# A windowed-attention network on one core: one pipeline over all tiles, a transposed attention product, normalisation moved to another engine

## The chip, the core and the metric

The kernel runs on one core of a Trainium2 chip. A core has five engines with instruction streams of their own: TensorE (PE, matrix products into PSUM), VectorE (DVE), ScalarE (ACT), GpSimd (POOL) and SyncE (SP, here for DMAs). They meet at semaphores. The metric is the device time of one execution in microseconds. About 0.5% is what a measurement of this kernel can tell from no change.

## What is computed

Three parts: a retention layer, a network of six layers of windowed attention with gated FFN, and a second layer with attention and a mixture of experts. The change is in the network alone, on x of shape (4, 512, 128):

```python
for i in range(DEPTH):                        # 6
    x = attn_layer(shift_tokens(x), Wqkv[i], q_scale[i], k_scale[i], Wo[i]) + x
    x = ffn_layer(shift_tokens(x), ln_g[i], ln_b[i], W1[i], b1[i], W2[i], b2[i]) + x
...
def attn_layer(x, Wqkv, qs, ksc, Wo):         # 16 heads of 64
    q, k, v = jnp.split(x @ Wqkv, 3, -1)
    q = l2norm(q) * qs
    k = l2norm(k) * ksc
    q = q * cos * scale + rotate_half(q) * sin * scale
    k = k * cos * inv + rotate_half(k) * sin * inv
    out = local_attention(q, k, v)            # windows of 32 queries, 64 keys
    return out @ Wo
...
sim = jnp.einsum('bhwie,bhwje->bhwij', bq, bk2) * QK_SCALE
attn = jax.nn.softmax(jnp.where(mask, -jnp.finfo(sim.dtype).max, sim), -1)
out = jnp.einsum('bhwij,bhwje->bhwie', attn, bv2)
...
return a * jax.nn.gelu(gate, approximate=False) @ W2 + b2
```

Everything is f32 but the mask product, which is bf16.

## The kernel before

`build_retention` runs first, then `build_network`, then `build_second_layer`; each is a block of its own. In `build_network` the unit of work is a tile of 128 tokens. A batch has four tiles (`s` or `t`, 0 to 3), a round is one layer of one batch, and there are 6 x 4 = 24 rounds, 96 tiles. A round's four stages handle tile `s` at lag 0, and work of earlier tiles at lag 1 and 2 (`Round.tile`). One stage of TensorE (`pe_round`) has:

- at lag 0, the projections: four matmuls of 512 columns for q and k into `qk_ps` (L393), two for v into the ring (L380);
- at lag 1, sixteen transposes of the normalised `qkn` in four bursts (L404), the mask product (L418) and the scores (L423), 64 small matmuls in two halves, into `sc_ps`;
- at lag 2, eight transposes of the exponentials `pe_` (named `pexp` in the profile, L438), the attention product (L453) in two halves, also into `sc_ps`, and eight transposes of its normalised output `o_tok` (L467).

In the attention product the stationary operand is `prT`, 64 keys by 32 queries of one head, and the moving one is `v_win`, 64 keys by 64 columns. Its output has the queries on the partitions, so it is transposed before the output projection.

VectorE (`dve_round`) rotates q and k out of `qk_ps` (L708, L713), sums the squares that ScalarE made (L721), floors them (L726), does a Newton step on the inverse norms (`newton_step`, L733 to L737), takes maxima and subtracts them (L742, L747), sums the exponentials and takes the reciprocal (L755, L757), and multiplies the attention output by it (`normalise`, L767). GpSimd adds the two rotary terms in two halves (L352) and multiplies by the inverse norms in two halves (L359). ScalarE copies what comes out of the ring (L564), squares (L575), makes the exponentials (L613) and the inverse norms (L580, L584), and runs GELU (L603), for which it loads another table and then the first one again. SyncE loads weights and moves V into windows, 16 DMAs per tile.

All transposes, v and the FFN go through `ring`, two PSUM banks filled in turn in the order of a list written out by hand (`order`); `bank_free` makes each fill wait for the reader of the fill two before. The FFN of round r runs in round r + 1: the output projection (L475, eight matmuls of 512 columns, each of two records), `add_attention` (L776), centring and variance (L481, L486) in stage 2; the up projections of gate and linear part (L493, L495), GELU, `ffn_gated` (L789), the down projection (L502) and `add_ffn` (L796) in stage 3. `ffn_norm` (L781, L783) ends stage 2 on VectorE.

A matmul of f32 shows as two records, a transpose as one. PSUM tile `sc_ps` is used in turn: scores of tile t (lag 1), maxima and subtraction on VectorE, attention product of tile t (lag 2, next stage), `normalise` on VectorE, scores of the next tile. The waits on both sides are these two lines, in `scores` and in `attend`:

```python
pe.wait_ge(o_ready.sem, o_ready.at(it, 2 * t))
...
pe.wait_ge(sc_sub.sem, sc_sub.at(it, 2 * (t + 1)))
```

## Time and profile before

| | us |
|---|---|
| runs of the kernel before: lowest, median, highest of 3 | 2250.7, 2259.16, 2259.73 |
| the profiled execution: its own time | 2256.97 |
| its span, first to last instruction | 2255.2 |
| mean granted TensorE clock | 0.972 of full |
| TensorE busy (matmul) | 1958.2 (87%) |
| VectorE busy | 1561.8 (69%) |
| ScalarE busy | 1151.2 (51%) |
| GpSimd busy | 863.9 (38%) |

The busy time of TensorE counts matmuls that overlap once, and their modelled ends; the distance between the starts of two successive groups is the better measure of what a group costs. In a timeline row the columns are start, duration, engine, line, operation, output<-inputs, stationary shape, moving shape, number of records, and in brackets the idle time ahead of the first of them with what ended it.

### The profile page before, as it was taken

The numbers are of one execution on the slowest core, as the hardware profiler recorded it, in microseconds if no ns is written. First come the engines' busy times: TensorE is split into PE (matmuls) and PEld (weight loads), VectorE is DVE, ScalarE is ACT, GpSimd is POOL, SyncE is SP. The second block draws the span as 40 slices with busy tenths as digits, with TensorE's granted clock in tenths as the row PEclk, the third lists the DMA queues.
The fourth block names the chain that finished last, engine by engine and source line by source line (L and its number), as shares of the span: only waits on it lengthen the run. The fifth ranks groups of instructions, "written<-read, shape, count | busy, mean of one in ns | idle before, by whom it ended". The sixth has DMA issues, their size and how long they took to land. (4 is left out here: it accounts for less than half of the span.)

```text
span 2255.2 us, 71087 instructions
## 1 busy us (share of the span) xinstructions
PE 1958.2 (87%) x31016; PEld 1121.9 (50%) x31016; DVE 1561.8 (69%) x2095; ACT 1151.2 (51%) x1934; POOL 863.9 (38%) x427
## 2 busy tenths in 40 slices
PE   6858889889989898989889898899988888986898
PEld 5635455455545544554555454455544545543444
DVE  6648777777767877777777777778777777863443
ACT  4425555554655555455555555555555555553234
POOL 0225444444434534444443444444445444430000
PEclk9979999999999999999999999999999999997788
DMA  1023222223222322222232222232223222221000
GB/s 42 1 72 93 48 54 60 73 58 75 54 46 56 87 66 58 55 51 67 62 79 50 57 57 74 49 75 62 50 56 86 66 49 56 60 52 43 0 9 10
DMA packets 83885, 124.96 MB, mean 55 GB/s; under 512 B 26112, under 2 KB 31880, under 8 KB 82704
## 3 DMA queue, kind: packets, MB, share of 16 engines
q1 hardware_dynamic: 83600, 120.64, 22.2%
q8 instruction: 242, 3.96, 0.8%
q14 instruction: 43, 0.35, 0.1%
HBM read 21.98 MB, written 1.05 MB: 10 GB/s over the span
## 5 line engine op out<-in xcount | busy, mean ns | idle before, releaser
L352 POOL TENSOR_TENSOR t<-t 128x1024 f32<-128x1024 f32 x192 | 453.3, 2361 | 661.4 <-DVE t L713 661.4
L359 POOL TENSOR_TENSOR qkn<-t,rn 128x1024 f32<-128x1024 f32 x192 | 374.2, 1969 | 373.9 <-DVE rn L737 373.9
L393 PE MATMUL qk_ps<-wqkv,state 128*128 128x512 f32 x768 | 396.5, 599 | 11.5 <-DMA wqkv<-in_w_qkv 9.2
L708 DVE TENSOR_TENSOR t<-qk_ps,rot 128x1024 f32<-128x1024 f32 x192 | 234.5, 1222 | 195.4 <-ACT sq L575 135.5
L404 PEld LDWEIGHTS ring<-ident,qkn 128*128 128x128 f32 x1536 | 180.9, 141 | 198.9 <-issue 122.0
L404 PE MATMUL ring<-ident,qkn 128*128 128x128 f32 x1536 | 233.8, 278 | 26.2 <-POOL qkn L359 25.6
L713 DVE TENSOR_TENSOR t<-qk_ps,rot 128x1024 f32<-128x1024 f32 x192 | 233.1, 1214 | 0.0
L721 DVE TENSOR_REDUCE lnsum<-sq 128x16 f32<-128x1024 f32 x192 | 231.8, 1208 | 0.0
L564 ACT COPY prT<-ring 128x512 f32<-128x512 f32 x192 | 113.2, 590 | 217.2 <-PE ring L438 217.2
L575 ACT ACTIVATE sq<-qk_ps 128x1024 f32<-128x1024 f32 x192 | 198.0, 1031 | 39.0 <-PE qk_ps L393 38.0
L564 ACT COPY oT<-ring 128x512 f32<-128x512 f32 x192 | 112.6, 586 | 184.0 <-PE ring L467 184.0
L380 PE MATMUL ring<-wqkv,state 128*128 128x512 f32 x384 | 200.4, 624 | 3.6 <-DMA wqkv<-in_w_qkv 2.7
L423 PE MATMUL sc_ps<-kT,qT 64*32 64x64 f32 x12288 | 170.6, 224 | 23.9 <-issue 23.9
L423 PEld LDWEIGHTS sc_ps<-kT,qT 64*32 64x32 f32 x12288 | 135.9, 105 | 83.1 <-issue 82.8
L475 PE MATMUL ring<-oT,wo 128*128 128x512 f32 x384 | 170.7, 598 | 0.7 <-ACT oT L564 0.7
L453 PE MATMUL sc_ps<-v_win,prT 64*32 64x64 f32 x12288 | 168.1, 225 | 2.7 <-issue 1.6
L564 ACT COPY v_tok<-ring 128x512 f32<-128x512 f32 x192 | 112.1, 584 | 113.3 <-PE ring L380 113.3
L453 PEld LDWEIGHTS sc_ps<-v_win,prT 64*32 64x32 f32 x12288 | 135.6, 106 | 63.9 <-issue 62.3
L564 ACT COPY qT<-ring 128x512 f32<-128x512 f32 x192 | 111.4, 580 | 104.7 <-PE ring L404 104.7
L742 DVE TENSOR_REDUCE smax<-sc_ps 128x16 f32<-128x1024 f32 x96 | 117.2, 1221 | 68.1 <-PE sc_ps L423 68.1
L438 PE MATMUL ring<-ident,pexp 128*128 128x128 f32 x768 | 120.0, 279 | 29.5 <-ACT pexp L613 20.4
L438 PEld LDWEIGHTS ring<-ident,pexp 128*128 128x128 f32 x768 | 87.8, 140 | 111.0 <-issue 74.7
(235 smaller groups left out, 2727.2 us busy)
## 6 DMA issues: line engine op xcount, KB each, us to landing
v_win<-v_tok SPq DMA_DIRECT2D x1488, 64.0 KB, 2.0
wqkv<-in_w_qkv SPq DMA_DIRECT2D x6, 1024.0 KB, 5.6
wqkv<-in_w_qkv SPq DMA_DIRECT2D x6, 512.0 KB, 3.7
wo<-in_w_o SPq DMA_DIRECT2D x6, 512.0 KB, 3.8
w<-in_w SPq DMA_DIRECT2D x6, 341.0 KB, 4.0
w<-in_w SPq DMA_DIRECT2D x6, 192.0 KB, 3.9
r_xtok<-in_x SPq DMA_DIRECT2D x4, 256.0 KB, 4.0
amask<-in_att_mask SPq DMA_DIRECT2D x1, 1024.0 KB
```

The costliest lines, as they stand in the source:

```text
L352: nc.gpsimd.tensor_tensor(t1[:, to], t1[:, to], t2[:, to], ALU.add).then_inc(qk_added.sem, 1)
L359: nc.gpsimd.tensor_tensor(qkn[:, to].rearrange("p (h d) -> p h d", d=DH), t1[:, to].rearrange("p (h d) -> p h d", d=DH), rn[:, HEADS * hal ...
L380: nc.tensor.matmul(to, tile_of(r, s), wqkv[:, 2 * INNER + 512 * par:2 * INNER + 512 * (par + 1)], start=True, stop=True).then_inc(v_full.s ...
L393: nc.tensor.matmul(qk_ps[:, c, :], tile_of(r, s), wqkv[:, 512 * c:512 * (c + 1)], start=True, stop=True).then_inc(qk_full.sem, 1)
L404: ins = nc.tensor.transpose(to[:, n * P:(n + 1) * P], qkn[:, c * P:(c + 1) * P], ident[:, :])
L423: ins = nc.tensor.matmul(sc_ps[WIN * q:WIN * (q + 1), par, 64 * pair:64 * (pair + 1)], qT[64 * par:64 * (par + 1), pair, WIN * q:WIN * (q ...
L438: ins = nc.tensor.transpose(to[:, n * P:(n + 1) * P], pe_[:, c * P:(c + 1) * P], ident[:, :])
L453: ins = nc.tensor.matmul(sc_ps[WIN * q:WIN * (q + 1), par, DH * pair:DH * (pair + 1)], prT[64 * par:64 * (par + 1), pair, WIN * q:WIN * (q ...
L564: nc.scalar.copy(to, bank_of(r, (what, s, lag, f))).then_inc(done.sem, 1)
L708: nc.vector.tensor_tensor(t1[:, to].rearrange("p (h d) -> p h d", d=DH), own, rot[:, 2 * half, s:s + 1, :].to_broadcast([P, HEADS, DH]), A ...
L713: nc.vector.tensor_tensor(t2[:, to].rearrange("p (h s d) -> p h s d", s=2, d=DH // 2), swapped, rot[:, 2 * half + 1, s:s + 1, :].to_broadc ...
L721: nc.vector.tensor_reduce(lnsum[:, HEADS * half:HEADS * (half + 1)], sq[:, INNER * half:INNER * (half + 1)].rearrange("p (h d) -> p h d", ...
```

## The change

The order by rounds becomes one loop over stages g = 0 to 101, in Python on every engine, so that GpSimd's and SyncE's instruction streams are written out too. Stage g has the projections of tile g, the qkn transposes and scores of tile g - 1, the P transposes of g - 2 and the attention product of g - 3. Row maxima and row sum of tile g - 2 stand at the head of VectorE's stage g.

The FFN of a round is spread over stages (by g modulo 4): up projections with GELU in 0, down projection and first half of the output projection (now two halves of 256 columns) in 1, second half in 2, centring, variance and norm in 3.

The attention product has `v_win` (64 keys by 64 columns) as its stationary operand and `prT` (64 keys by 32 queries) as its moving one, and writes head columns by queries, straight into the two ring banks; ScalarE copies them to `oT`. `transpose_o`, `o_tok` and `normalise` are gone. In their place GpSimd multiplies the exponentials by `rden` ahead of the transposes (`scale_p`, two halves of 512 columns).

The Newton step and the floor are on GpSimd (`inverse_norms`, five operations on 128x32), which also scales q and k in four quarters of 512 columns where it did two halves; ScalarE makes its own floored copy (`raised`, one more small activation). The rotary tables have two buffers. The output projection's weights are loaded apart from the FFN's.

TensorE's order at the end of a plain stage and the head of the next, before (L467 transposes `o_tok`, L418 is the mask product, L453 is the attention product):

```order
L380 MATMUL ring<-wqkv,state 128x512 [waits qkT_copied] x2
L418 MATMUL sc_ps<-mask_bf,ident_bf 128x512 [waits o_ready,qkT_copied]
L418 MATMUL sc_ps<-mask_bf,ident_bf 128x512
L423 MATMUL sc_ps<-kT,qT 32x64 x32
L467 MATMUL ring<-ident,o_tok 128x128 [waits v_copied,o_ready]
L467 MATMUL ring<-ident,o_tok 128x128 x3
L423 MATMUL sc_ps<-kT,qT 32x64 x32
L467 MATMUL ring<-ident,o_tok 128x128 [waits v_copied,o_ready]
L467 MATMUL ring<-ident,o_tok 128x128 x3
L393 MATMUL qk_ps<-wqkv,state 128x512 [waits q_sq]
```

and in the change, at the end of a stage with g modulo 4 = 1 and the head of the next (L423 transposes `pn`, L404 is the mask product, L409 the scores, L440 the attention product, L370 and L379 project q and k, L392 transposes qkn):

```order
L404 MATMUL sc_ps<-mask_bf,ident_bf 128x512 [waits sc_sub,qkT_copied]
L404 MATMUL sc_ps<-mask_bf,ident_bf 128x512
L409 MATMUL sc_ps<-kT,qT 32x64 x32
L423 MATMUL ring<-ident,pn 128x128 [waits v_copied,p_scaled]
L423 MATMUL ring<-ident,pn 128x128 x3
L409 MATMUL sc_ps<-kT,qT 32x64 x32
L440 MATMUL ring<-prT,v_win 64x32 [waits pT_copied,v_moved3]
L440 MATMUL ring<-prT,v_win 64x32 x31
L370 MATMUL qk_ps<-wqkv,state 128x512 [waits q_rot,q_sq]
L440 MATMUL ring<-prT,v_win 64x32 x32
L370 MATMUL qk_ps<-wqkv,state 128x512
L392 MATMUL ring<-ident,qkn 128x128 [waits oT_copied,qk_scaled]
```

The P transposes moved to the place of the output's, the attention product to the head of the stage; the scores wait for the subtraction (`sc_sub`) where they waited for `o_ready`.

GpSimd's work for one tile, before:

```order
L352 TENSOR_TENSOR t<-t 128x1024 [waits qk_rot]
L350 REGISTER_ALU
L352 TENSOR_TENSOR t<-t 128x1024 [waits qk_rot]
L353 REGISTER_ALU
L354 REGISTER_ALU [waits qk_added]
L359 TENSOR_TENSOR qkn<-t,rn 128x1024 [waits qkT_full,rn_ready]
L359 TENSOR_TENSOR qkn<-t,rn 128x1024
```

and in the change, from one stage's inverse norms on:

```order
L295 TENSOR_SCALAR ss<-sums 128x32 [waits sums_ready]
L297 TENSOR_TENSOR nw<-rs 128x32 [waits rs_ready]
L299 TENSOR_TENSOR nw<-nw,ss 128x32 [waits newton]
L301 TENSOR_SCALAR nw<-nw 128x32 [waits newton]
L303 TENSOR_TENSOR rn<-nw,rs 128x32 [waits newton]
L311 TENSOR_TENSOR qkn<-qkn,rn 128x512 [waits q_added,rn_ready]
L311 TENSOR_TENSOR qkn<-qkn,rn 128x512
L311 TENSOR_TENSOR qkn<-qkn,rn 128x512 [waits k_added]
L311 TENSOR_TENSOR qkn<-qkn,rn 128x512
L328 TENSOR_TENSOR pn<-pexp,rden 128x512 [waits pT_full,rden_ready]
L328 TENSOR_TENSOR pn<-pexp,rden 128x512
L320 TENSOR_TENSOR qkn<-t 128x1024 [waits qkT_full,q_rot]
```

Four instructions for a tile became thirteen, and the additions (L320) now stand behind the scaling of two earlier tiles.

VectorE's order in a plain stage, before, from the maxima on:

```order
L742 TENSOR_REDUCE smax<-sc_ps 128x16 [waits sc_full]
L747 TENSOR_TENSOR pr<-sc_ps,smax 128x2x4x64 [waits max_ready]
L747 TENSOR_TENSOR pr<-sc_ps,smax 128x2x4x64
L708 TENSOR_TENSOR t<-qk_ps,rot 128x1024 [waits qk_full,qk_scaled]
L713 TENSOR_TENSOR t<-qk_ps,rot 128x1024
L755 TENSOR_REDUCE den<-pexp 128x16 [waits exp_ready]
L757 RECIPROCAL rden<-den 128x16 [waits den_ready]
```

and in the change:

```order
L670 TENSOR_REDUCE smax<-sc_ps 128x16 [waits sc_full]
L677 TENSOR_TENSOR pr<-sc_ps,smax 128x2x4x64 [waits exp_ready,max_ready]
L677 TENSOR_TENSOR pr<-sc_ps,smax 128x2x4x64
L684 TENSOR_REDUCE den<-pexp 128x16 [waits exp_ready]
L689 RECIPROCAL rden<-den 128x16 [waits p_scaled,den_ready]
L704 TENSOR_TENSOR t<-qk_ps,rot 128x1024 [waits q_added,q_full]
L708 TENSOR_TENSOR t<-qk_ps,rot 128x1024
```

The row sum now follows the subtraction at once, with the rotations behind it; the wait of the subtraction for `exp_ready` is for the tile before.

The core of the diff:

```diff
+        def stage_fills(g):
+            now, turn, prob, att = (tile_there(g - n) for n in range(4))
+            up, down = round_at(g, 0, 2), round_at(g, 1, 2)
+            out_0, out_1, centre = round_at(g, 1, 1), round_at(g, 2, 1), round_at(g, 3, 1)
+            fills = []
+            fills += [("a", g - 3, f) for f in range(2)] * att
+            fills += [("xc", centre, 0)] * (centre is not None)
+            fills += [("t", g - 1, 0)] * turn
+            fills += [("w2", down, 0)] * (down is not None)
+            fills += [("t", g - 1, 1)] * turn
+            fills += [(k, up, 0) for k in ("gate", "lin")] * (up is not None)
+            fills += [("t", g - 1, 2)] * turn
+            fills += [("v", g, 0)] * now
+            fills += [(k, up, 1) for k in ("gate", "lin")] * (up is not None)
+            fills += [("t", g - 1, 3)] * turn
+            fills += [("wo", out_0, 0)] * (out_0 is not None)
+            fills += [("var", centre, 0)] * (centre is not None)
+            fills += [("v", g, 1)] * now
+            fills += [("wo", out_1, 1)] * (out_1 is not None)
+            fills += [(k, up, 2) for k in ("gate", "lin")] * (up is not None)
+            fills += [("p", g - 2, f) for f in range(2)] * prob
+            return fills
...
+                def inverse_norms(g):
+                    pool.wait_ge(sums_ready, 2 * (g + 1))
+                    nc.gpsimd.tensor_scalar(ss[:, :], sums[:, :], NORM_FLOOR, None, ALU.max).then_inc(newton, 1)
+                    pool.wait_ge(rs_ready, g + 1)
+                    nc.gpsimd.tensor_tensor(nw1[:, :], rs[:, :], rs[:, :], ALU.mult).then_inc(newton, 1)
+                    pool.wait_ge(newton, 4 * g + 2)
+                    nc.gpsimd.tensor_tensor(nw2[:, :], nw1[:, :], ss[:, :], ALU.mult).then_inc(newton, 1)
+                    pool.wait_ge(newton, 4 * g + 3)
+                    nc.gpsimd.tensor_scalar(nw3[:, :], nw2[:, :], -0.5 * LN_SCALE * LN_SCALE ** 0.5, 1.5 * LN_SCALE ** 0.5, ALU.mult, ALU.add).then_inc(newton, 1)
+                    pool.wait_ge(newton, 4 * g + 4)
+                    nc.gpsimd.tensor_tensor(rn[:, :], nw3[:, :], rs[:, :], ALU.mult).then_inc(rn_ready, 1)
+                    pool.wait_ge(rn_ready, g + 1)
...
+                def scale_p(g, f):
+                    if f == 0:
+                        pool.wait_ge(rden_ready, g + 1)
+                        if g > 0:
+                            pool.wait_ge(pT_full, 2 * g)
+                    nc.gpsimd.tensor_tensor(by_head(quarter(pn, f)), by_head(quarter(pe_, f)),
+                                            rden[:, 8 * f:8 * (f + 1)].unsqueeze(2).to_broadcast([P, 8, DH]), ALU.mult).then_inc(p_scaled, 1)
...
+                for g in range(TILE_COUNT + 2):
+                    if tile_there(g - 1):
+                        inverse_norms(g - 1)
+                        for f in range(4):
+                            scale_qk(g - 1, f)
+                    if tile_there(g - 2):
+                        for f in range(2):
+                            scale_p(g - 2, f)
+                    if tile_there(g):
+                        for k in range(2):
+                            add_terms(g, k)
...
+                        pe.wait_ge(pT_copied, 2 * (g + 1))
+                        pe.wait_ge(v_moved[t], moves_of[t] * (g // TILES + 1))
+                        for part in range(2):
+                            ring_bank("a", g, part)
+                    for pair in range(2 * f, 2 * (f + 1)):
                         for q in range(TW):
                             for par in range(2):
-                                ins = nc.tensor.matmul(
-                                    sc_ps[WIN * q:WIN * (q + 1), par, DH * pair:DH * (pair + 1)],
-                                    prT[64 * par:64 * (par + 1), pair, WIN * q:WIN * (q + 1)],
-                                    v_win[64 * par:64 * (par + 1), TW * t + q, DH * pair:DH * (pair + 1)],
-                                    start=True, stop=True)
+                                n = 2 * pair + par
+                                for part in range(2):
+                                    ins = nc.tensor.matmul(
+                                        to[part][64 * par:64 * (par + 1), P * pair + WIN * q:P * pair + WIN * (q + 1)],
+                                        v_win[64 * part:64 * (part + 1), TW * t + q, DH * n:DH * (n + 1)],
+                                        prT[64 * part:64 * (part + 1), n, WIN * q:WIN * (q + 1)],
+                                        start=True, stop=True)
...
-                        pe.wait_ge(o_ready.sem, o_ready.at(it, 2 * t))
+                        pe.wait_ge(qkT_copied, 4 * (g + 1))
+                        if g > 0:
+                            pe.wait_ge(sc_sub, 2 * g)
...
+                for g in range(STAGES):
+                    now, turn, prob, att = (tile_there(g - n) for n in range(4))
+                    up, down = round_at(g, 0, 2), round_at(g, 1, 2)
+                    out_0, out_1, centre = round_at(g, 1, 1), round_at(g, 2, 1), round_at(g, 3, 1)
+                    for f in range(2):
+                        if att:
+                            attend(g - 3, f)
+                        if now:
+                            project_q(g, f)
+                    if centre is not None:
+                        ffn_centre(centre)
+                    if turn:
+                        transpose_qk(g - 1, 0)
+                    if down is not None:
+                        ffn_down(down)
+                    if now:
+                        project_k(g, 0)
+                    if turn:
+                        transpose_qk(g - 1, 1)
+                    if now:
+                        project_k(g, 1)
+                    if up is not None:
+                        ffn_up(up, 0)
+                    if turn:
+                        transpose_qk(g - 1, 2)
+                    if now:
+                        project_v(g, 0)
+                    if up is not None:
+                        ffn_up(up, 1)
+                    if turn:
+                        transpose_qk(g - 1, 3)
+                    if out_0 is not None:
+                        output_projection(out_0, 0)
+                    if centre is not None:
+                        ffn_variance(centre)
+                    if now:
+                        project_v(g, 1)
+                    if out_1 is not None:
+                        output_projection(out_1, 1)
+                    if up is not None:
+                        ffn_up(up, 2)
+                    for f in range(2):
+                        if prob:
+                            transpose_p(g - 2, f)
+                        if turn:
+                            scores(g - 1, f)
...
+                    if prob:
+                        row_max(g - 2)
+                        row_sum(g - 2)
+                    if now:
+                        rotate(g, 0)
+                    if up is not None:
+                        ffn_gated(up, 0)
+                    if down is not None:
+                        add_ffn(down)
+                    if now:
+                        rotate(g, 1)
+                    if up is not None:
+                        ffn_gated(up, 1)
+                    if now:
+                        sum_squares(g, 1)
+                        sum_squares(g, 0)
+                    if up is not None:
+                        ffn_gated(up, 2)
+                    if out_0 is not None:
+                        add_attention(out_0, 0)
+                    if out_1 is not None:
+                        add_attention(out_1, 1)
+                    if centre is not None:
+                        ffn_norm(centre)
```

## Rows read from the trace of the kernel before

**Rows 1.** The page, part 1: busy us, share of the span, instructions

```profile
PE 1958.2 (87%) x31016; PEld 1121.9 (50%) x31016; DVE 1561.8 (69%) x2095; ACT 1151.2 (51%) x1934; POOL 863.9 (38%) x427
```

**Rows 2.** Timeline of TensorE, one plain stage (start, us, instructions)

```profile
598.64 1.02 PE L393 MATMUL qk_ps<-wqkv,state 128*128 128x512 f32 x2
599.51 0.60 PE L404 MATMUL ring<-ident,qkn 128*128 128x128 f32 x4
...
604.50 0.86 PE L453 MATMUL sc_ps<-v_win,prT 64*32 64x64 f32 x64
605.28 0.66 PE L404 MATMUL ring<-ident,qkn 128*128 128x128 f32 x4
...
610.11 0.59 PE L418 MATMUL sc_ps<-mask_bf,ident_bf 128*128 128x512 bf16 x2 [1.47 <-DVE o_tok L767]
...
611.42 0.66 PE L467 MATMUL ring<-ident,o_tok 128*128 128x128 f32 x4
612.00 0.86 PE L423 MATMUL sc_ps<-kT,qT 64*32 64x64 f32 x64
612.79 0.66 PE L467 MATMUL ring<-ident,o_tok 128*128 128x128 f32 x4
613.29 1.02 PE L393 MATMUL qk_ps<-wqkv,state 128*128 128x512 f32 x2
```

**Rows 3.** Timeline of TensorE, the stages of tiles 2 and 3

```profile
629.36 0.30 PE L423 MATMUL sc_ps<-kT,qT 64*32 64x64 f32 x4 [1.35 <-issue]
...
630.08 1.02 PE L393 MATMUL qk_ps<-wqkv,state 128*128 128x512 f32 x2
...
632.68 7.03 PE L475 MATMUL ring<-oT,wo 128*128 128x512 f32 x16
...
654.10 1.02 PE L393 MATMUL qk_ps<-wqkv,state 128*128 128x512 f32 x2
...
678.11 1.02 PE L393 MATMUL qk_ps<-wqkv,state 128*128 128x512 f32 x2
```

**Rows 4.** Timeline, TensorE's first and VectorE's last work in the network

```profile
141.82 6.53 PE L393 MATMUL qk_ps<-wqkv,state 128*128 128x512 f32 x8 [9.23 <-DMA wqkv<-in_w_qkv]
...
2073.13 1.53 DVE L796 SCALAR_TENSOR_TENSOR state<-ring,col,xa 64x512 f32<-64x512 f32 x2 [2.94 <-PE ring L502]
```

**Rows 5.** Timeline of TensorE, retention part, 64-column matmuls behind 128-column weights

```profile
116.52 3.68 PE L1061 MATMUL pd<-vsb,at 128*128 128x64 f32 x32
```

**Rows 6.** Groups by line, 500 to 1000 us: busy, mean ns | idle before

```profile
L352 POOL TENSOR_TENSOR t<-t 128x1024 f32<-128x1024 f32 x51 | 120.5, 2362 | 178.2 <-DVE t L713 178.2
...
L359 POOL TENSOR_TENSOR qkn<-t,rn 128x1024 f32<-128x1024 f32 x50 | 97.4, 1970 | 103.8 <-DVE rn L737 103.8
L708 DVE TENSOR_TENSOR t<-qk_ps,rot 128x1024 f32<-128x1024 f32 x51 | 62.3, 1222 | 46.7 <-ACT sq L575 35.4 <-POOL qkn L359 7.4 <-PE qk_ps L393 2.0
...
L721 DVE TENSOR_REDUCE lnsum<-sq 128x16 f32<-128x1024 f32 x50 | 60.4, 1208 | 0.0
L575 ACT ACTIVATE sq<-qk_ps 128x1024 f32<-128x1024 f32 x51 | 52.6, 1031 | 6.7 <-PE qk_ps L393 6.7
...
L747 DVE TENSOR_TENSOR pr<-sc_ps,smax 128x512 f32<-128x512 f32 x50 | 32.2, 686 | 0.9
...
L783 DVE TENSOR_SCALAR xn<-xc,col 128x512 f32<-128x512 f32 x6 | 12.0, 2007 | 0.2
...
L603 ACT ACT_TABLE_LOAD x7 | 9.0, 1283 | 0.1
...
L580 ACT ACTIVATE lnss<-ss 128x32 f32<-128x32 f32 x25 | 5.7, 230 | 29.3 <-DVE ss L726 29.2
```

**Rows 7.** Two GpSimd products: xcount, ns min/median/max, first and last start

```profile
L341 POOL TENSOR_TENSOR rot<-rot_base,qks x24: 719/728/743, 145.1 to 1709.8; 128x256 f32<-128x256 f32 x24
...
L974 POOL TENSOR_TENSOR kst<-rqk,rdec x4: 1717/1768/1769, 39.3 to 106.7; 128x512 f32<-128x512 f32 x4
```

**Rows 8.** Timeline of GpSimd, the affine select at the start

```profile
1.18 0.29 POOL L966 TENSOR_SCALAR_AFFINE_SELECT r_ident<-r_ident 128x128 f32<-128x128 f32 x1 [0.23 <-POOL r_ident L964]
```

886 lines of the change are left out of this document (372 added, 514 removed).

## Prediction

> **What bounds the kernel now.** I read the page's first part first [rows 1]: TensorE is busy for 87% of the span and no other engine reaches 70%. A share of busy time hides gaps, so next I read TensorE's timeline of one stage, from the first projection of a tile to the first projection of the next: 598.64 to 613.29 us, 14.65 us [rows 2]. Two successive starts give what a piece really takes: 0.87 us for one 512-column f32 projection (598.64 to 599.51), 0.79 us for half of the attention product (604.50 to 605.28, 64 records), 0.58 and 0.50 us for the two bursts that transpose its output, `o_tok` (611.42 to 612.00, 612.79 to 613.29). One row has an idle time: at 610.11 TensorE has waited 1.47 us for VectorE's `o_tok`, because the scores of the next tile use the same PSUM tile as the attention product. So a plain stage is 13.18 us of TensorE work (I count drains and small gaps in) and 1.47 us of waiting.
>
> The stages with FFN work are another case [rows 3]. Those of tile 2 (630.08 to 654.10) and of tile 3 (654.10 to 678.11) take 24.0 us each. Their FFN work is 8 matmuls of the output projection (6.9 us, the row at 632.68) and 11 others of 0.87 us: 16.4 us per round of four tiles. Four tiles of 13.18 and 16.4 make 69.1 us, and the round from 598.64 to 678.11 took 79.5. About 10 us per round is waiting, most of it in the two long stages, where projection, centring, variance, up and down projection follow each other inside one stage and each waits for ScalarE or VectorE. One pause of 1.35 us (the row at 629.36, "issue") belongs to no engine; I take 1.2 us of such pauses per round and keep them.
>
> The network runs from 141.8 to 2074.7 us (2073.13 + 1.53) [rows 4], 1932.9 us; the 322 us around it are not touched.
>
> **Part by part, on TensorE.** (1) The output's transposes go: 0.58 + 0.50 = 1.08 us per tile. (2) The wait for `o_tok` goes, since the attention product now lands in the ring's banks; what the scores wait for instead is VectorE's subtraction of the tile before, which ends some 7 us earlier in the stage (a reduction of 1.21 and two products of 0.69 from the stage's start). (3) The attention product is turned round: as many matmuls (64 per tile, 128 records), but the stationary operand is now 64x64 of `v_win` where it was 64x32 of `prT`, and 32 columns are streamed where there were 64. Streaming halves, and half as many regions of the array are in use, so that cancels. The weight load does not. The row that prices it is in the retention part: 32 matmuls of 64 columns behind 128-column weights take 3.68 us [rows 5], less the last one's 0.28 that is 0.110 us each, twice what 64 columns need by the 0.87 us of two 512-column records. So they go at the pace of their weight loads: 0.86 ns per weight column, 55 ns for 64 columns, 27 for 32. Today 64 records start in 0.86 - 0.22 = 0.64 us, 10 ns each, so about three loads of 27 ns proceed side by side, in eight regions. In four regions a record would take 55/4 = 13.8 ns if loads hide the streaming, (55 + 27)/4 = 20.5 ns if they add to it: +0.5 to +1.3 us per tile. Lower bound of the whole item 0 (issue alone sets 10 ns); upper bound 45 ns a record more, 5.8 us per tile, if no two loads overlap. I take +0.85, near the ends that the eight regions of today support.
>
> The Trainium skill speaks against this edit: "TensorE: Matmul & The Clock Gate", Part 3, The mechanism, says that a weight load overlaps running matmuls only where its row group differs. Here there are two row groups, so by that rule loads would go two at a time; the 10 ns of today are less than half of 27, so the trace does not bear the rule out for column regions. By the rule the sum would end near 2245, no change (rival C).
>
> So a tile costs TensorE 13.18 - 1.08 + 0.85 = 12.95 us.
>
> (4) FFN work is spread. Of each four stages the first gets the up projections (six matmuls, 5.2 us), the second the down projection and half of the output projection (2.6 + 3.45), the third the other half (3.45), the fourth centring and variance (1.7). TensorE's work: 18.1, 19.0, 16.4, 14.7 us. Stalls that remain, worked out from offsets within the stage: in the first, the third `qkn` transpose takes the bank of the first gate. That is freed by a GELU, which stands on ScalarE behind the squares of k (1.03; k is projected at 6.9, after two halves of the attention product, 2.4, four projections and two transposes, so they end at 8.1) and a table load of 1.28 [rows 6]: free at 10.1, wanted at 8.6, 1.5 us. The last up projection waits for a V copy that stands behind the squares of q, 0.9 us; and VectorE enters this stage late (below), 0.8. Together 21.3 us. In the second, the first P transpose waits for the addition that frees the output projection's bank: 19.5. The others 16.5 and 14.9. With 1.2 of pauses a round is **73.4 us** against 79.5.
>
> **The other engines** [rows 6]. VectorE loses the normalisation (two products like L747's 0.69) and four small operations; it keeps per tile four rotations of 1.22, four reductions of 1.21 and the two subtractions of 0.69: 11.1 us and a reciprocal, in 14.9 at the least. In the fourth stage it ends with the FFN norm, whose second instruction alone takes 2.0 (L783), so it starts the next stage late. ScalarE, now at 51% [rows 1], loses nothing and gains one activation of 0.23. SyncE keeps its 16 V moves per tile and their place; the loads of a layer's weights stand behind waits that are over a stage before their turn, so they hold nothing up, and V's weights, behind the moves, could come late five times in all.
>
> GpSimd gets the load: two additions of 2.36, four scalings of q and k at 128x512 instead of two at 1024 columns, two scalings of P, five operations on 128x32. The trace has the 1024-column scaling with the same broadcast at 1.97 (L359) and a 256-column product at 0.73 [rows 7]: a line from 0.73 at 256 to the 2.36 of L352 at 1024 leaves a fixed part of 0.18, so (1.97 + 0.18)/2, some 1.05 us, for 512, and 0.25 for 32. Bounds for 512: 0.98 (half of 1.97) and 1.77, the row of `kst`, which reads slices of wider rows; I stay with 1.05, since P and qkn are contiguous. The small operations: not under a fixed part of 0.18, at most the 0.73 of the 256-column row. Each of the four hand-overs between dependent ones costs 0.23, the idle time before the affine select [rows 8]. Sum: 4.7 + 6.3 + 1.3 + 0.9 = **13.2 us per tile**, up from 8.6, and under the 14.9 of the shortest stage: covered, with 1.7 us to spare.
>
> What counts is the latency. ScalarE's inverse norms stand behind its P copies, which end as TensorE's stage ends. From there: three activations of 0.23 with hand-overs, 0.8; four small operations and hand-overs on GpSimd, 1.9; the first quarter's scaling, 1.05: ready 3.8 us into the stage. TensorE gets to that transpose after two halves of the attention product (1.2 each now) and two projections (0.87), at 4.2. The cover is 0.4 us thin; beyond it each microsecond on GpSimd costs 96.
>
> **Sum.** The first 8 stages have only the first output projections and centring: 8 x 13.1 (the tile's 12.95 with little to wait for) + 6.9 + 1.7 = 113 us. 22 rounds of 73.4: 1615. The six last stages drain: two P and two attention products, the FFN of one round and a half, each waiting for the one before; by their TensorE work 30 us, with VectorE's and ScalarE's part laid end to end about twice that; I take 60. Together 1788, 145 us less than 1932.9. The profiled execution's 2256.97 becomes **2112**; the median shown is 2.2 above it, which I leave out.
>
> **Rivals.** (A) The wider loads are hidden entirely: 0.85 less per tile, 82 us: 2030. For it: today's bursts may be limited by issue. Against it: the 110 ns row. 15%.
> (B) Latency or the two-bank ring eats the gain. If each small GpSimd operation takes 0.73, the first quarter is ready at 5.7, 1.5 late in each of 96 stages: 2256. If a scaling of 512 columns takes 1.77, GpSimd needs 17.5 us, so the two shorter stages grow by 3.6 per round: about 2195. If the first two stages stay at 24 and 22 us because their ring fills wait as they do now: 2225. Against it: none of these rows has the form that is used. 16%, 2 of it within 0.5%.
> (C) Slower: the 64-wide loads do not overlap between regions. The forecast has 16.6 ns a record (10 and 0.85 us/128). Break-even is where a tile costs 1.5 us (145/96) more than forecast, 28 ns; loads in pairs (27.5) end there, near 2245, and one by one (55) cost 4.9 us more on each of 96 tiles: 2580. For it: in the retention part one load follows another at 110 ns. Against: the 10 ns of today. 10% for slower, 2% for pairs.
>
> **Numbers.** Forecast 57%, its own range 2060 to 2170. Less than 0.5% of the time is about what a measurement here can't tell from none. Faster 0.86 (forecast, A, most of B), same 0.04, slower 0.10. Range 2000 to 2225: A is mostly in, B up to its ring case, C out.
>
> **What would show it.** The attention product's burst of 64 records at about 1.25 us (A: 0.86; C: above 1.9). No idle time before the mask matmul. GpSimd busy for 55 to 62% of the span and its small operations at 0.25. The first qkn transpose of a stage with no long wait on GpSimd. Stages of about 21, 19.5, 16.5 and 15 us. VectorE near 64%. Wrong would be: four stages of equal length (GpSimd or a cycle through it sets the pace), or the first two still near 24.

## The result and the profile after

The changed kernel takes **2225.3 us** (median of 4 runs, 2218.0 to 2231.5) beside 2258.5 for the kernel before: ratio 0.985, 95% interval 0.981 to 0.989. It is faster, as forecast, but by 33 us where 145 were forecast, and the time lies 0.3 us above the upper end of the range. The page's first part, against [rows 1]:

```profile
span 2229.8 us, 70852 instructions
...
PE 1949.5 (87%) x30532; PEld 1195.8 (54%) x30632; DVE 1347.5 (60%) x1564; ACT 1181.8 (53%) x2030; POOL 1198.6 (54%) x1291
```

TensorE's share is unchanged at 87%. VectorE and GpSimd have changed places, and neither is near a bound. The timeline of TensorE over two short stages (tiles with g mod 4 = 2 and 3), from the attention product of one to that of the next, against [rows 2]:

```profile
1485.34 0.86 PE L409 MATMUL sc_ps<-kT,qT 64*32 64x64 f32 x64
1486.12 0.66 PE L423 MATMUL ring<-ident,pn 128*128 128x128 f32 x4
1486.71 0.86 PE L409 MATMUL sc_ps<-kT,qT 64*32 64x64 f32 x64
1487.55 1.14 PE L440 MATMUL ring<-prT,v_win 64*64 64x32 f32 x64
1488.61 1.13 PE L370 MATMUL qk_ps<-wqkv,state 128*128 128x512 f32 x2
1489.67 1.14 PE L440 MATMUL ring<-prT,v_win 64*64 64x32 f32 x64
1490.73 1.13 PE L370 MATMUL qk_ps<-wqkv,state 128*128 128x512 f32 x2
1491.70 0.60 PE L392 MATMUL ring<-ident,qkn 128*128 128x128 f32 x4
...
1496.14 0.62 PE L392 MATMUL ring<-ident,qkn 128*128 128x128 f32 x4 [0.39 <-ACT kT L555]
...
1504.27 1.14 PE L440 MATMUL ring<-prT,v_win 64*64 64x32 f32 x64
...
1520.09 0.64 PE L409 MATMUL sc_ps<-kT,qT 64*32 64x64 f32 x39 [0.45 <-issue]
1520.67 1.14 PE L440 MATMUL ring<-prT,v_win 64*64 64x32 f32 x64
```

From 1487.55 to 1504.27 is 16.72 us, to 1520.67 another 16.40. The stage of the up projections that follows took 21.9 and the one of the down projection ahead of these 20.8: 75.9 for that round. Over the 22 full rounds (from the attention product of stage 8, at 263.13, to that of stage 96, at 1987.21) a round took 78.4 on average, and its four stages 22.4, 21.4, 17.8 and 16.8 where 21.3, 19.5, 16.5 and 14.9 were forecast. A half of the attention product goes at 1.06 us (1489.67 to 1490.73). Nothing is idle before the mask matmul. TensorE's waits, whole execution (us in total, times, longest):

```profile
PE ring L440 <- issue: 63.5, 76, 2.1
PE ring L392 <- ACT gel L609: 34.2, 23, 1.5
PE ring L392 <- ACT kT L555: 28.1, 73, 0.4
PE sc_ps L409 <- issue: 15.1, 28, 1.1
PE ring L423 <- ACT xsq L600: 10.4, 23, 0.5
PE ring L384 <- DVE gel L742: 8.4, 25, 0.4
```

The longest item is a wait for nothing that the profile knows: "issue", inside the bursts of small matmuls, 78.6 us for the attention product and the scores together. I call these waits pauses. In the kernel before they were some 25 us. They fall into the chain of four bursts from 1485.34 on, which the change has put next to each other: scores, four transposes, scores, attention product, one projection, attention product. That is 128 small matmuls, which show as 256 records of matmuls and as many of weight loads.

### The profile page after: what moved, and what is told of

It is laid out like the page before. It is cut to its first block and busy times, and to the rows that moved or that the text cites. A ratio compares the mean times of both kernels' runs of the same rounds, so it can differ in the third digit from the quotient of the medians.

```text
span 2229.8 us, 70852 instructions
## 1 busy us (share of the span) xinstructions
PE 1949.5 (87%) x30532; PEld 1195.8 (54%) x30632; DVE 1347.5 (60%) x1564; ACT 1181.8 (53%) x2030; POOL 1198.6 (54%) x1291
## 3 DMA queue, kind: packets, MB, share of 16 engines
HBM read 21.98 MB, written 1.05 MB: 10 GB/s over the span
## 5 line engine op out<-in xcount | busy, mean ns | idle before, releaser
L320 POOL TENSOR_TENSOR qkn<-t 128x1024 f32<-128x1024 f32 x192 | 451.8, 2359 | 195.9 <-PE ring L392 118.5
L311 POOL TENSOR_TENSOR qkn<-qkn,rn 128x512 f32<-128x512 f32 x384 | 388.2, 1042 | 7.5
L392 PEld LDWEIGHTS ring<-ident,qkn 128*128 128x128 f32 x1536 | 181.7, 142 | 311.7 <-issue 265.1
L392 PE MATMUL ring<-ident,qkn 128*128 128x128 f32 x1536 | 237.9, 278 | 68.8 <-ACT gel L609 34.2
L440 PE MATMUL ring<-prT,v_win 64*64 64x32 f32 x12288 | 241.3, 222 | 64.5 <-issue 63.5
L440 PEld LDWEIGHTS ring<-prT,v_win 64*64 64x64 f32 x12288 | 213.7, 136 | 156.2 <-issue 144.6
L684 DVE TENSOR_REDUCE den<-pexp 128x16 f32<-128x1024 f32 x96 | 117.1, 1220 | 258.9 <-ACT pexp L546 258.9
L328 POOL TENSOR_TENSOR pn<-pexp,rden 128x512 f32<-128x512 f32 x192 | 196.2, 1043 | 120.7 <-DVE rden L689 120.5
L370 PE MATMUL qk_ps<-wqkv,state 128*128 128x512 f32 x384 | 224.4, 669 | 14.4 <-DMA wqkv<-in_w_qkv 8.0
L718 DVE TENSOR_REDUCE sums<-sq 128x16 f32<-128x1024 f32 x192 | 226.2, 1210 | 3.3 <-ACT sq L576 2.9
L546 ACT ACTIVATE pexp<-pr 128x512 f32<-128x512 f32 x192 | 121.3, 632 | 157.9 <-DVE pr L677 157.9
L379 PE MATMUL qk_ps<-wqkv,state 128*128 128x512 f32 x384 | 199.2, 601 | 0.0
L297 POOL TENSOR_TENSOR nw<-rs 128x32 f32<-128x32 f32 x96 | 22.9, 238 | 327.6 <-ACT rs L588 327.6
L409 PE MATMUL sc_ps<-kT,qT 64*32 64x64 f32 x12288 | 172.9, 224 | 15.3 <-issue 15.1
```

The source lines that it names most:

```text
L311: nc.gpsimd.tensor_tensor(by_head(quarter(qkn, f)), by_head(quarter(qkn, f)), rn[:, 8 * f:8 * (f + 1)].unsqueeze(2).to_broadcast([P, 8, DH ...
L320: nc.gpsimd.tensor_tensor(half(qkn, k), half(t1, k), half(t2, k), ALU.add).then_inc((q_added, k_added)[k], 1)
L328: nc.gpsimd.tensor_tensor(by_head(quarter(pn, f)), by_head(quarter(pe_, f)), rden[:, 8 * f:8 * (f + 1)].unsqueeze(2).to_broadcast([P, 8, D ...
L370: nc.tensor.matmul(qk_ps[:, f, :], tile_of(g), quarter(wqkv, f), start=True, stop=True).then_inc(q_full, 1)
L379: nc.tensor.matmul(qk_ps[:, 2 + f, :], tile_of(g), quarter(wqkv, 2 + f), start=True, stop=True).then_inc(k_full, 1)
L392: ins = nc.tensor.transpose(to[:, n * P:(n + 1) * P], qkn[:, c * P:(c + 1) * P], ident[:, :])
```

## The experiments

The ratios are to the kernel before, measured beside each of them: 2257.9 to 2259.7 us. Small differences between kernels are judged by their ranges, which are 5 to 10 us wide. I tested these theories. **F**: the instructions of the four adjacent bursts are not supplied fast enough. **D**: the bytes of the V moves are in the way. **L**: the wider weight loads are the cost. **G**: GpSimd's load or latency is. **O**: the pauses belong to the form of the attention product alone. Another was that the waits for ScalarE's copies are the cost.

### Narrow loads in the new place

```
-    to[part][64*par:64*(par+1), P*pair + WIN*q:P*pair + WIN*(q+1)],
-    v_win[64*part:64*(part+1), TW*t + q, DH*n:DH*(n+1)],
-    prT[64*part:64*(part+1), n, WIN*q:WIN*(q+1)],
+    to[part][WIN*q:WIN*(q+1), DH*n:DH*(n+1)],
+    prT[64*part:64*(part+1), n, WIN*q:WIN*(q+1)],
+    v_win[64*part:64*(part+1), TW*t + q, DH*n:DH*(n+1)],
```

> The changed kernel with one edit: the attention product's operands are swapped back (weights 64x32 of prT, 64 columns of v_win streamed), in the new place in the pipeline. Its output is left untransposed, so that what follows is not the attention output; every later instruction is there and has the size it had. Theory L (the wider weight loads cost what the sum took, 0.85 us per tile): about 80 us less than the changed kernel, some 2145; a burst of 64 attention records from 1.14 down to about 0.8. Theory F (the pauses called issue inside the four bursts of small matmuls come because the engine runs through these instructions faster than they arrive): only 30 to 50 us less, since faster bursts pause more; idle time put down to issue grows from 87 to over 110 us. Theory Z (the loads cost nothing, the stage is set by waits): 2225.

Measured: 2211.0 (2206.6 to 2217.0), ratio 0.978. That is 14 us less, not 80, and below even the 30 to 50 of theory F. The group's row (busy us, mean ns, idle before it), first of the changed kernel, then of this one:

```profile
L440 PE MATMUL ring<-prT,v_win 64*64 64x32 f32 x12288 | 241.3, 222 | 64.5 <-issue 63.5 <-ACT prT L566 0.8
```

```profile
L440 PE MATMUL ring<-v_win,prT 64*32 64x64 f32 x12288 | 212.6, 222 | 78.8 <-issue 77.8 <-ACT prT L566 0.8
```

What the bursts gain (29 us), the pauses take back by half (14). Faster bursts pause more, as F says, and the width of the loads explains only a small part of the missing gain.

### Large matmuls between the bursts

```
+    project_q(g, 0); project_q(g, 1)
     attend(g - 3, 0)
-    project_q(g, 0)
+    project_k(g, 0)
     attend(g - 3, 1)
-    project_q(g, 1)
+    project_k(g, 1)
     ...
     transpose_qk(g - 1, 0)
-    project_k(g, 0)
     transpose_qk(g - 1, 1)
-    project_k(g, 1)
```

> The changed kernel with TensorE's order edited: both q projections come before the attention product, and the k projections behind its first and its second half, so that four large matmuls stand between and around the bursts that were adjacent (scores, scores, attention, attention). Nothing is left out. Theory F (pauses come where more than some 300 small matmuls follow each other closely): idle time put down to issue falls from 87 to under 45 us, and the time by 30 to 50, to about 2185, unless the transposes, which lose the projections between them, wait more for ScalarE. Theory D (pauses come from DMA traffic of the V moves, which fall into the same stretch): the issue time stays near 87, the time within 10 us of 2225. Theory O (a property of the attention form alone): stays as well.

Measured: 2269.3 (2264.9 to 2277.3), ratio 1.005: 44 us slower than the changed kernel. The attention product's pauses did what F says, the rest did not. The rows of the attention product and of the qkn transposes:

```profile
L392 PE MATMUL ring<-ident,qkn 128*128 128x128 f32 x1536 | 235.5, 278 | 131.4 <-ACT gel L608 41.9 <-DVE state L748 32.1 <-ACT kT L554 18.6
L440 PE MATMUL ring<-prT,v_win 64*64 64x32 f32 x12288 | 218.0, 220 | 2.9 <-issue 2.1 <-ACT prT L565 0.8
```

The attention product lost its pauses (64.5 to 2.9 us idle, and 23 us of busy time: a record of 222 ns covers the first part of each pause, whose neighbours start 17 ns apart otherwise). The scores, whose surroundings are as before, kept theirs (15.3 us). But the transposes' idle time went from 68.8 to 131.4: without a projection between them they meet a two-bank ring whose copies are not done, and in the stage of the down projection they wait 1.5 us for VectorE's addition. So the projections were cover for the ring. O falls, since the attention product has the form that it had, and the cure has to leave that cover.

### V moves of 8 columns

```
-    of = v_tok[WIN*q:WIN*(q+1), g % 2, part, :]
+    of = v_tok[WIN*q:WIN*(q+1), g % 2, part, 0:8]
```

The two destinations are cut alike, and `v_win` is cleared at the start.

> The changed kernel with V moves of 8 columns instead of 512: as many DMAs and the same waits, 1/64 of the bytes; the rest of v_win is zero, so the attention output is mostly zero. Theory D (the V moves' bytes delay the fetching of instructions): idle time put down to issue falls from 87 to under 40 us and the half-clock stretches in the network go; time about 2170. Theory F (the density of small matmuls alone): 87 +- 10 us stay, time within 10 us of 2225.

Measured: 2220.7 (2212.2 to 2223.4), ratio 0.982. The windows 500 to 1000 us (busy of each engine, granted clock, DMA share, GB/s) and the waits:

```profile
500.00:1000.00 500.00, 448.49 (x7916) 271.77 (x7928) 318.05 (x353) 283.59 (x494) 312.64 (x340) 1.00 0.05 11
```

```profile
PE ring L440 <- issue: 56.4, 73, 1.8
...
PE sc_ps L409 <- issue: 18.8, 28, 1.1
```

The DMA engines' share fell from 0.25 to 0.05, and 75 us of the 79 us of pauses stayed. D falls, as far as it is about bytes: the number of the moves is the same.

### ScalarE's squares of k later

```
-    squares(g, 1)
     gelu(up, 0)
     copy_qkT(g - 1, 2)
+    squares(g, 1)
     copy_v(g, 0)
```

> The changed kernel with ScalarE's order edited: the squares of k stand behind the first GELU and behind the copy of the third qkn transpose. Nothing is left out. If the two waits (28 us of L392 for the copy into kT, 34 us of L392 for the first GELU) are worth their length: up to 60 us less, about 2165 to 2180. If the squares, and with them VectorE's k rotation, the sums and the next tile's inverse norms, become what is late: 2225 or above. I expect about 2185, with a new wait of a few tenths of a us for the V copy or GpSimd.

Measured: 2262.0 (2254.9 to 2271.8), ratio 1.002: 37 us slower than the changed kernel. The wait for `kT` went, but three others came for the V copy behind the squares, and the first one here grew from 8.4:

```profile
PE ring L384 <- DVE gel L742: 20.8, 24, 1.0
PE ring L384 <- ACT v_tok L562: 18.5, 27, 0.7
PE ring L455 <- ACT v_tok L562: 17.8, 23, 0.8
PE ring L464 <- ACT v_tok L562: 17.8, 23, 0.8
```

In this ring of two banks moving a copy's lateness away from one place brought it to the next ones. My expectation had the new wait at "a few tenths"; it was 0.7 to 0.8 us where it occurred, and it occurred three times a round.

### P not normalised

GpSimd's two products per tile are left out, and `transpose_p` reads `pe_` and waits for the exponentials.

> The changed kernel without the normalisation of P: its transposes read the exponentials, GpSimd's two products of 512 columns per tile are gone (2.1 us of its 12.5 per tile), the reciprocal is still worked out. The attention output is unnormalised. Theory: GpSimd has slack and sets nothing: within 8 us of 2225. The rival: GpSimd's load or its latency costs the missing gain: 2225 less 40 or more.

Measured: 2238.2 (2226.9 to 2238.5), ratio 0.992. GpSimd's busy time fell from 1198.6 to 1004.4 us and nothing was gained: G falls as far as it is about load. The loss of 13 us beside 2225, more than the 8 that I had allowed, I cannot explain; the profiled execution has the same waits and spans 2225.1.

### Half of the scores left out

```
-    for par in range(2):
+    for par in range(1):
         ins = nc.tensor.matmul(sc_ps[...], qT[...], kT[...])
```

> The changed kernel with every second score matmul left out (those of the odd heads; their scores are the mask alone): 64 instead of 128 per tile, 256 instead of 512 records of small matmuls in front of the attention product, which is as it was. Theory F: the pauses between the attention product's matmuls go, from a mean of 0.47 us per half to under 0.1, 90 us, besides what the left-out matmuls take themselves (at most 0.8 us per tile): 2225 - 90 - 60 = about 2075. The rival (the pauses belong to the attention product's own instructions or to its place beside ScalarE's and the DMAs' work): they stay and the time falls by the left-out matmuls alone, at most 75 us: 2150 or more.

Measured: 2106.5 (2101.7 to 2107.2), ratio 0.933: 119 us less.

```profile
L440 PE MATMUL ring<-prT,v_win 64*64 64x32 f32 x12288 | 223.0, 220 | 21.7 <-ACT prT L566 18.4 <-issue 2.7
L409 PE MATMUL sc_ps<-kT,qT 64*32 64x64 f32 x6144 | 124.8, 219 | 0.0
```

The attention product is untouched, its pauses are gone (63.5 to 2.7 us, and 18 us of busy time with them), because fewer instructions stand in front of it. In its place it waits 18.4 us for the copy of P, which the pauses had hidden. The left-out matmuls themselves account for 48 us (172.9 - 124.8), the other 71 us of the gain are pauses, less that new wait; the rival allowed 75 in all. F holds: what counts is how many instructions come close together. (In front of the attention product of a tile there were 256 records of score matmuls and their loads, and 128 are left; the 512 and 256 of the expectation are too many.)

### Narrow loads where there are no pauses

The order of the second experiment with the operands of the first.

> The order of the run in which the projections stand apart (2269), where the attention product has no pauses and half of it takes 1.065 us, now with the narrow weight loads (64x32 of prT as weights, 64 columns of v_win streamed; output left untransposed, wrong for what follows). If the wider loads are what makes a half 1.065 instead of the 0.79 of the kernel before: 0.27 us less for each of 192 halves, 52 us: 2217. If the place is: unchanged, 2265.

Measured: 2236.7 (2233.4 to 2240.7), ratio 0.991, 33 us less than with wide loads. A half takes 0.94 us, which accounts for 23 of them (busy time 194.8 for 218.0):

```profile
1489.63 1.01 PE L440 MATMUL ring<-v_win,prT 64*32 64x64 f32 x64
1490.57 1.12 PE L379 MATMUL qk_ps<-wqkv,state 128*128 128x512 f32 x2
```

That is between the two expectations, 0.79 (the width) and 1.065 (the place). The run with eight regions in turn, further down, tells why.

### The order that keeps both covers

```
     transpose_qk(g-1, 0); ffn_down; transpose_qk(g-1, 1)
     project_k(g, 1)
     ... (as before)
+    scores(g - 1, 0)
     transpose_p(g - 2, 0)
-    scores(g - 1, 0)
     transpose_p(g - 2, 1)
     scores(g - 1, 1)
+    project_q(g + 1, 0)
     attend(g - 2, 0)
-    project_q(g + 1, 0)
-    attend(g - 2, 1)
     project_q(g + 1, 1)
+    attend(g - 2, 1)
+    project_k(g + 1, 0)      (was behind the first qkn transposes)
```

On ScalarE both exponentials stand ahead of the two output copies.

> The changed kernel with TensorE's order edited so that more large instructions stand among the small matmuls, and the transposes keep a projection between them: first half of the scores, both P transposes, second half of the scores, q projection, first half of the attention product, q projection, second half, k projection; on ScalarE both exponentials come before the two output copies. Nothing is left out. Theory F (the dense stretch from the first scores to the end of the attention product takes some 7.0 us however little work is in it, because its 512 instructions arrive no faster): work that is moved in there is free, so the stretch stays near 7.1 us with 6.7 us of work and a tile gains about 0.8 us: 2150. The other side: what is moved uncovers waits of the transposes for ScalarE's copies, as in the run with the projections ahead of the attention product: 2190 to 2240.

Measured: **2135.5 us** (2132.1 to 2136.3), ratio 0.946, 95% interval 0.944 to 0.948: 90 us faster than the changed kernel, with every instruction the same. How much of it is due to ScalarE's order was not measured apart. The timeline and the rows of the two bursts:

```profile
1483.39 0.86 PE L409 MATMUL sc_ps<-kT,qT 64*32 64x64 f32 x64
1484.18 1.09 PE L423 MATMUL ring<-ident,pn 128*128 128x128 f32 x8
1485.20 0.95 PE L409 MATMUL sc_ps<-kT,qT 64*32 64x64 f32 x64
1486.09 1.13 PE L370 MATMUL qk_ps<-wqkv,state 128*128 128x512 f32 x2
1487.14 1.14 PE L440 MATMUL ring<-prT,v_win 64*64 64x32 f32 x64
1488.21 1.13 PE L370 MATMUL qk_ps<-wqkv,state 128*128 128x512 f32 x2
1489.26 1.14 PE L440 MATMUL ring<-prT,v_win 64*64 64x32 f32 x64
1490.33 1.12 PE L379 MATMUL qk_ps<-wqkv,state 128*128 128x512 f32 x2
```

```profile
L440 PE MATMUL ring<-prT,v_win 64*64 64x32 f32 x12288 | 220.8, 220 | 3.9 <-issue 2.9 <-ACT prT L568 0.8
...
L409 PE MATMUL sc_ps<-kT,qT 64*32 64x64 f32 x12288 | 171.8, 224 | 0.4 <-issue 0.3
```

The stretch from the first scores to the end of the attention product takes 6.94 us here and holds one projection (two records) and four transposes more than the 5.39 us of the changed kernel (1485.34 to 1490.73). But that was one of its few undisturbed stretches. Counted with the mask in front, the changed kernel's stretches have a mean of 7.0 us and run from 5.7 to over 8; with half of the scores left out most take 5.5, and here most take 7.15 to 7.35. So the work moved in was nearly free: it stands where pauses were.

The pauses themselves are waits for instructions, and the DMA packets of the traces show it. The last column of this row of the changed kernel is a share of the DMA engines' time, the others are packets and MB; the second row is of the kernel with half of the scores left out:

```profile
q8 instruction: 240, 3.93, 0.8%
```

```profile
q8 instruction: 192, 3.15, 0.7%
```

These are packets of 16 KB. Leaving out 6,144 records of matmuls and as many loads took away 48 of them, so one packet holds 256 instructions of TensorE (240 x 256 is 61,440, beside 61,164 records of matmuls and loads in the trace). The trace has the start and the length of each. One started at 573.41 and ended at 574.34; this pause ended 1.54 us later:

```profile
573.28 0.89 PE L440 MATMUL ring<-prT,v_win 64*64 64x32 f32 x47
575.88 0.55 PE L440 MATMUL ring<-prT,v_win 64*64 64x32 f32 x17 [1.70 <-issue]
```

Between 160 and 1850 us the changed kernel has 98 listed pauses, and 94 of them end 1.15 to 1.65 us after the end of such a packet; of its 178 other waits 4 do. In the kernel before all 27 do, and the number of matmuls and loads started ahead of each of the 27 leaves the same remainder by 256 (215 or 216): each pause stands at the seam of two packets. The row at 629.36 that the prediction read is one of them. No two packets of any run started less than 3.2 us apart inside the network, which makes at most 80 instructions per microsecond over a longer time. A short stretch can be faster (the undisturbed one has 528 in 5.39 us, 98 per microsecond) as long as no seam is reached before its packet.

### The GELU before the squares, and its table early

On top of the reordered kernel, two edits of ScalarE's stage with up projections. First:

```
+    gelu(up, 0)
     squares(g, 1)
-    gelu(up, 0)
```

> The reordered kernel (2135) with one more edit on ScalarE: in the stage with the up projections the first GELU comes before the squares of k. Nothing is left out. If the 1.5 us that a qkn transpose waits for that GELU in each of 23 stages is worth its length, and the V copies behind stay where they are: 15 to 30 us less, 2105 to 2120. The other side: the squares of k end 1 us later there, and VectorE's rotation of k, its gating product or the second transposes' copy become late: 2135 to 2160.

Measured: 2137.5 (2131.6 to 2138.2), ratio 0.945: the same. The wait for the GELU went only from 34.1 to 30.2 us; the squares were not what it stood behind. Then, instead:

```
     exponentials(g - 2, 0); exponentials(g - 2, 1)
+    nc.scalar.preload_act_table_set("gelu_and_others")
     copy_o(g - 3, 0)
```

> The reordered kernel (2135) with one more edit on ScalarE: in the stage with the up projections the GELU's table is loaded behind the exponentials, where ScalarE waits for the attention product anyway, and not in front of the first GELU. Nothing is left out. If the table load of 1.28 us is what makes a qkn transpose wait 1.49 us for the first GELU in each of 23 stages: the wait falls to some 0.3 us and the time by 20 to 27, to about 2110. If TensorE then waits as long for the next thing (GELU of the second part, V copies): 2130 to 2137, as with the GELU ahead of the squares.

Measured: **2119.4 us** (2114.3 to 2123.7), ratio 0.937, 95% interval 0.934 to 0.940, the fastest of the kernels here that leave nothing out. The wait for the first GELU is gone; of its 34 us the time shows 16, since TensorE waits 9 us more for V's weights (14.9 for 6.2) and 4 more for VectorE's gating products (11.7 for 7.6). So it was the table load of 1.28 us in front of the first GELU, and this wait was worth half its length, a little less than the 20 to 27 us expected.

### Narrow loads, eight regions in turn

On the reordered kernel, with the operands of the first experiment and:

```
-    for q in range(TW):
-        for par in range(2):
-            n = 2 * pair + par
+    for par in range(2):
+        n = 2 * pair + par
+        for q in range(TW):
             for part in range(2):
```

> The reordered kernel (2135) with the attention product in the form of the kernel before (weights 64x32 of prT, 64 columns of v_win streamed), its matmuls in an order in which eight in a row use the eight different regions of the array; output left untransposed, wrong for what follows. A half took 0.789 us in the kernel before, 0.945 in the run with narrow loads where only four regions alternate, 1.065 with wide loads. If the number of regions in turn sets the pitch: 0.79 for a half, 0.28 x 192 = 53 us less, 2082, unless the denser bursts bring the pauses back (then 2095 to 2125). If the place in the program sets it: 0.945, 2112.

Measured: 2102.5 (2100.6 to 2106.2), ratio 0.929, 33 us less than the reordered kernel. A half takes 0.79 us, as before the change:

```profile
1484.87 0.86 PE L440 MATMUL ring<-v_win,prT 64*32 64x64 f32 x64
1485.65 1.12 PE L370 MATMUL qk_ps<-wqkv,state 128*128 128x512 f32 x2
1486.71 0.86 PE L440 MATMUL ring<-v_win,prT 64*32 64x64 f32 x64
```

```profile
L440 PE MATMUL ring<-v_win,prT 64*32 64x64 f32 x12288 | 175.6, 224 | 14.9 <-issue 13.3 <-ACT prT L568 0.8
```

So the number of regions in turn sets the pitch: 0.79 with eight, 0.94 with the same weights where the next four matmuls share a column region. The busy time prices the wide form against this one: 220.8 - 175.6 = 45 us, of which new pauses (14.9 for 3.9) take back 11.

### The norms 2.1 us later on GpSimd

```
+    for f in range(2):
+        nc.gpsimd.tensor_tensor(pn[:, 512*f:512*(f+1)], qkn[...], nw3[...] (to 512 columns), ALU.mult)
     nc.gpsimd.tensor_tensor(rn[:, :], nw3[:, :], rs[:, :], ALU.mult)
```

> The changed kernel (2225) with two more products of 512 columns on GpSimd, into pn, right before the last operation of the inverse norms, so that the first scaled quarter of q comes 2.1 us later; nothing is left out. In a plain stage of the changed kernel the quarter is ready 1.1 us before TensorE turns to it. The prediction's claim (beyond the cover each microsecond costs each of 96 tiles as much): 1.0 x 96 less what longer stages hide, 60 to 95 us: 2285 to 2320. The rival (the lateness is taken up by waits and pauses that are there anyway): within 20 us of 2225.

Measured: 2251.4 (2244.0 to 2259.3), ratio 0.996: 26 us more, between the two expectations. TensorE's wait for `qkn`:

```profile
PE ring L398 <- POOL qkn L317: 20.5, 15, 5.5
```

Only 15 waits are listed and their sum is 20.5 us; in the changed kernel they were 3 and 5.6. Over all tiles the first scaled quarter of the changed kernel is ready 2.4 us (median) before its transpose starts, against 1.1 in the undisturbed stage above: pauses and longer stages give cover. In 34 of the 96 tiles the distance is under 2.1 us, and what is missing there adds up to 20.6 us. So a microsecond costs about its length in each tile whose cover is used up, and nothing in the others. GpSimd's latency explains no more than those 5.6 us of the changed kernel's time, and G falls.

## Why the time was missed and the bound was not

**The bound** was right: TensorE, with its idle time, sets the end. The network's span is now 141.57 to 2049.20 us, 1907.6, against 1932.9 [rows 4] and 1788 forecast:

```profile
141.57 3.75 PE L370 MATMUL qk_ps<-wqkv,state 128*128 128x512 f32 x4 [7.96 <-DMA wqkv<-in_w_qkv]
...
2047.67 1.53 DVE L749 SCALAR_TENSOR_TENSOR state<-ring,col,xa 64x512 f32<-64x512 f32 x2 [2.94 <-PE ring L480]
```

**Items (1) and (2)**, the output's transposes and the wait for `o_tok`, went as forecast; nothing took the place of that wait before the mask (81.4 us of idle time before, 5.0 now).

**Item (3)**, the wider loads, was forecast at +0.85 us per tile, 82 us. Its reason was right and its size too large: the pitch of a half is 1.06 for 0.79, +0.54 per tile. Another +0.28 per tile has no term in the prediction: the projections of q and k are busy for 224.4 + 199.2 us against the 396.5 of the kernel before. Those that stand directly behind a burst of small matmuls take 1.06 or 0.97 us from start to start, for 0.87. The width of the burst's loads is not the reason, since in the run with eight regions in turn the distance is 1.06 as well (1485.65 to 1486.71) and the busy time 425.8; the place is. Together this makes 0.82, so the item came out by luck. The region argument is borne out by the run with eight regions in turn. The Trainium skill, "TensorE: Matmul & The Clock Gate", Part 3, The mechanism, lets a load overlap only where the row group differs. This does not describe what was measured: in the two runs with narrow loads the row groups alternate alike, and only the column regions' order differs, 0.94 against 0.79 us for 64 records. Rival C falls with it, and A too: the loads cost something.

**The pauses** are the step that failed: "One pause of 1.35 us (the row at 629.36, "issue") belongs to no engine; I take 1.2 us of such pauses per round and keep them." I read the pause as a property of the kernel that the change leaves alone. It was a property of the order: it came where bursts of small matmuls were close together, so that 256 instructions were used up before the next packet of them was there, and the change put the attention product right behind the scores. Before, transposes and projections stood between them. In the changed kernel the two listed idle times are 78.6 us, and the 241.3 us of the attention product hold another 20 against the 220.8 of the reordered kernel: about 99 where 29 were kept, 70 us too few. Half of the scores left out and the new order take the pauses away, the projections set apart take those of the attention product; V moves with fewer bytes, ScalarE's squares later and less work on GpSimd leave them.

**A consequence** was not in the sum either: after some of the long pauses the clock falls. Behind a pause of 1.70 us at 575.88 the windows (TensorE busy, granted clock, DMA share, GB/s) show

```profile
575.88:582.09 6.21, 6.21 (x86) 0.52 0.38 89
1487.55:1491.70 4.15, 4.15 (x135) 1.00 0.35 83
```

0.52 is the lower of the two levels, 1.2 of 2.4 GHz, against 1.00 in an undisturbed stage. There are four such stretches of 6.8 us in the middle of the network, behind pauses of 1.70, 1.32, 1.44 and 1.46 us; about 3.4 us are lost in each, 14 in all. Other pauses as long (1.51 us at 720.37, 1.43 at 801.32) had none behind them.

**Stage stalls (4).** The GELU's was forecast at 1.5 us and is 1.49 in each of 23 stages (34.2). V's copy and late VectorE in the first stage, 1.7 together, are 0.4 (8.4 us in 25). Not foreseen: the fourth qkn transpose waits 0.39 us for the copy into `kT`, which stands on ScalarE behind the squares of k (28.1 us), and small ones for `xsq` (10.4) and `oT` (7.1). Taken together +46 (28.1, 10.4 and 7.1) and -29 (1.3 us less in each of 22 rounds).

**GpSimd** was sized right: a 512-column product takes 1.04 (forecast 1.05), the small operations 0.22 to 0.36 on average (0.25), the hand-overs 0.08 (0.23). The page has 54% where 55 to 62 were forecast. The cover was wrong: in this stage it is 1.1 us, not 0.4, since the first quarter is ready at 1490.6 and wanted at 1491.70.

```profile
1488.32 0.24 POOL L297 TENSOR_TENSOR nw<-rs 128x32 f32<-128x32 f32 x1 [4.64 <-ACT rs L588]
...
1489.60 4.04 POOL L311 TENSOR_TENSOR qkn<-qkn,rn 128x512 f32<-128x512 f32 x4
```

Over all tiles its median is 2.4. The price of 96 per microsecond took the same thin cover for every tile; 2.1 us more cost 26 us, because only a third of the tiles ran out of cover. Rival B had the right time (2225 for its ring case) for a reason that holds in part only: ring waits are there, but the pauses are the larger part.

**The books.** The network came 120 us above the forecast: 9 in the first eight stages (121.6 for 113), 109 in the 22 rounds (78.4 for 73.4 each), 2 in the last six stages. By cause it is pauses 70, half clock 14, stage stalls 46 - 29: 101. Part of the 14 is in the busy time of the attention product and so in the 70 as well, which leaves 19 us or somewhat more untraced. The reordered kernel is at 1808.7, 21 above the forecast; its listed pauses are down to 3.2 us, and half of the low clock is left (three stretches of 3.4 to 6.8 us, behind waits of 1.3 to 1.9 us for V's weights). Its order exchanges some other waits as well, so this is no proof, but with the pauses out of the way the forecast of 2112 would have stood beside 2135, inside its own range of 2060 to 2170.

## What to carry to other kernels

Count how many instructions an order puts close together, weight loads included. Here TensorE's came in packets of 256, at least 3.2 us apart: four bursts of 64 records, each with its weight load, took 7.0 us on average where their work is 5.4 (5.7 with the mask), and large matmuls moved between them were nearly free. A large matmul between two transposes may be the cover of a small ring of banks, so choose those to move whose place behind is taken by another. A pause labelled "issue" in the profile of before is a reading about the order, and a change of order has to forecast it anew.

## What the runs showed of the hardware

- Bursts of 64x32 weights and 64 columns start a record every 12 ns where eight regions come in turn, every 15 where four matmuls in a row share a column region; bursts of 64x64 weights and 32 columns every 17 (0.79, 0.94 and 1.06 us for 64).
- TensorE's instructions were fetched in packets of 16 KB on a DMA queue of their own, 256 to a packet (240 packets; 192 with 12,288 instructions fewer). Each took 0.9 to 1.7 us, and no two started less than 3.2 us apart inside the network. Pauses of up to 2.1 us came at the seams of the packets and ended 1.15 to 1.65 us after a packet did, 94 of 98 in the changed kernel.
- A projection of two records directly behind a burst of small matmuls took 0.97 to 1.06 us from start to start, for 0.87 elsewhere, with 32-column and with 64-column weights in the burst.
- Pauses of 1.32 to 1.70 us had 6.8 us at half clock behind them in four places; others as long had none.
- GpSimd's 128x32 operations take 0.22 to 0.28 us (median), and dependent ones follow each other after 0.08.
- A GELU table loaded while ScalarE had nothing to do was worth 16 us in 23 stages (2135.5 to 2119.4).
